# First attention of a two-layer kernel: outputs sent through DRAM to the projection, and an unread 26-row product after the second scores

## What is computed

```python
qkv = x @ qkv_w + qkv_b
qkv = qkv.reshape(b, n, 3, H, D)              # b 16, n 512, H 16 heads, D 8
q, k, v = jnp.moveaxis(qkv, 2, 0)
attn = jnp.einsum('bnhd,bmhd->bhnm', q, k) * scale
attn = jax.nn.softmax(attn, axis=-1)
out = jnp.einsum('bhnm,bmhd->bnhd', attn, v).reshape(b, n, c)
out = out @ proj_w + proj_b                   # and x = x + out
```

## Time and profile before

| | us |
|---|---|
| median of 3 runs | 3365.65 |
| lowest, highest | 3340.04, 3366.84 |
| the profiled execution | 3353.67 |
| its span | 3351.9 |
| stretch of the first attention in it | about 460 to 1337 |
| mean granted TensorE clock over the span | 0.908 |

### The profile page before, as it was taken

The page is one execution under the profiler, slowest core; times in us unless marked ns, Lnnn a source line. Parts: engine busy times, 40 slices in busy tenths (PEclk is TensorE's granted clock), DMA queues, the critical chain, the costliest instruction groups (busy, mean ns, idle before and its releaser), DMA issues. The chain is left out here.

```text
span 3351.9 us, 46625 instructions
## 1 busy us (share of the span) xinstructions
PE 2934.7 (88%) x15938; PEld 1757.2 (52%) x15938; DVE 2516.6 (75%) x6115; ACT 1773.0 (53%) x2711; POOL 928.1 (28%) x885
## 2 busy tenths in 40 slices
PE   6999959999999998899995689899799999989853
PEld 4666623443443443666663556566566666656432
DVE  6888767888888880788876797867366778797765
ACT  3444406777777775444435556454345555555544
POOL 2221121121111100212101355556323323343333
PEclk9999957999999996899995689989899999999965
DMA  4343432122122110343430000000000000000000
GB/s 127 77 100 80 95 102 93 57 93 84 66 93 84 66 49 6 111 93 79 101 77 1 1 7 20 19 19 19 32 13 13 13 7 14 13 7 26 7 7 25
DMA packets 71588, 167.20 MB, mean 50 GB/s; under 512 B 8792, under 2 KB 9400, under 8 KB 67128
## 3 DMA queue, kind: packets, MB, share of 16 engines
q1 hardware_dynamic: 69176, 160.03, 16.5%
q10 hardware_dynamic: 2176, 4.19, 0.3%
HBM read 120.67 MB, written 43.52 MB: 49 GB/s over the span
## 5 line engine op out<-in xcount | busy, mean ns | idle before, releaser
L706 DVE TENSOR_REDUCE att_mx<-att_pair 128x2 f32<-128x1024 f32 x512 | 617.0, 1220 | 132.5 <-PE att_pair L955 132.1
L881 ACT ACTIVATE att_pt<-att_pair 128x1024 f32<-128x1024 f32 x512 | 522.8, 1025 | 235.7 <-PE att_pair L965 233.1
L977 PE MATMUL att_o<-att_pt,att_vx 128*32 128x256 f32 x4096 | 335.5, 413 | 9.8 <-ACT att_oT L887 5.1
L955 PE MATMUL att_pair<-att_k,att_q 24*128 24x512 f32 x1024 | 272.4, 535 | 48.8 <-DMA att_k<-att_spread_k 14.2
L965 PE MATMUL att_pair<-att_q,att_k 26*128 26x512 f32 x1024 | 265.5, 520 | 0.0
L965 PEld LDWEIGHTS att_pair<-att_q,att_k 26*128 26x128 f32 x1024 | 98.5, 191 | 195.0 <-issue 168.1
L457 ACT ACTIVATE ffnA_h<-ffnA_up,b 128x512 f32<-128x512 f32 x144 | 98.7, 686 | 178.9 <-PE ffnA_up L105 177.2
L457 ACT ACTIVATE ffnB_h<-ffnB_up,b 128x512 f32<-128x512 f32 x144 | 98.6, 685 | 178.1 <-PE ffnB_up L105 176.4
L955 PEld LDWEIGHTS att_pair<-att_k,att_q 24*128 24x128 f32 x1024 | 100.3, 195 | 136.2 <-ACT att_pt L881 89.2
L977 PEld LDWEIGHTS att_o<-att_pt,att_vx 128*32 128x32 f32 x4096 | 91.6, 111 | 143.0 <-issue 123.4
L1897 ACT ACTIVATE att1k_sq<-att1k_k 128x512 f32<-128x512 f32 x128 | 76.2, 595 | 165.0 <-PE att1k_k L105 164.9
(11 more groups left out here) (538 smaller groups left out, 7787.8 us busy)
## 6 DMA issues: line engine op xcount, KB each, us to landing
ffnA_weights<-ffnA_weights SPq DMA_DIRECT2D x128, 256.0 KB, 5.6
att_q<-att_spread_q SPq DMA_DIRECT2D x16, 1024.0 KB, 4.9
att_k<-att_spread_k SPq DMA_DIRECT2D x16, 1024.0 KB, 4.8
att_spread_q<-att_qhi SPq DMA_DIRECT2D x32, 256.0 KB, 2.5
att_spread_k<-att_khi SPq DMA_DIRECT2D x32, 256.0 KB, 3.3
twk_hi<-ffnB_weights SPq DMA_DIRECT2D x32, 256.0 KB, 3.9
twk_lo<-ffnB_weights SPq DMA_DIRECT2D x32, 256.0 KB, 5.0
tgk_hi<-ffnB_weights SPq DMA_DIRECT2D x32, 256.0 KB, 6.0
```

Source lines behind the costliest of these rows:

```text
L706: v.tensor_reduce(top[b % 2][:, t, h:h + 2], pair("s", k)[:, :].rearrange("p (h n) -> p h n", h=2), AX, ALU.max, negate=True).then_inc(mx, 1)
L881: a.activation(pt[k % 8][:, :, :].rearrange("p h n -> p (h n)"), pair("t", k)[:, :], ACT.Exp, scale=scale).then_inc(p_, 1)
L955: last = pe.matmul(pair("s", k)[:, (j - j0) * 512:(j - j0 + 1) * 512], qb[b % 3][r, u, t * P:(t + 1) * P], kb[b % 3][r, u, :], start=True, ...
L977: last = pe.matmul(obank[j * BLOCK:(j + 1) * BLOCK, cols], vxb[b % 3][:, t, 4 * u + j, :], pt[(2 * g + j // 2) % 8][:, j % 2, cols], start ...
```

## The change

The outputs are no longer turned on TensorE. ACT issues a DMA (`kept`, at 6, 14, 22, 30) that stores each unit's `oT` in DRAM, in `heads_o`, one row for each head and value. When a group's four units are there, SP (`gathered`) reads the 16 rows of sums as 128 x 64 and the 128 rows of numerators as 128 x 512. DVE takes the reciprocal of the sums at 19 (`inverted`), SP (`returned`) writes it to DRAM and reads it back with each head's row on eight partitions, and POOL multiplies into `ocol` (`divided`). The projection moves to 26, the addition to 28. With that `out`, `final` and their users are gone from the order of `misc`.

`misc_idle` lists for each step in which no user of `misc` is due the user that comes next: from two steps after a user to the step before the next. In a full group these are the steps 4, 7, 8, 11, 12, 15, 16, 19 to 25 and 28 to 33 (33 is step 1 of the next pass). There `keep_clock` runs one more matmul like the second scores, at row block 0, into `misc`, where nobody reads it. It stands between `again` and `scores`, and waits through `misc_free` as the next user would. POOL now runs the split of the next group's q and k before the norm of the group after it, and SP's queue takes `gathered` between the q and the k operands and `returned` behind the k operands.

```diff
     def uses_of_misc():
-        yield from (("x", 0), ("q", 0), ("k", 0), ("v", 0))
+        yield from ((-1, "x", 0), (-1, "q", 0), (-1, "k", 0), (-1, "v", 0))
...
             if now:
-                yield "maxima", m - 1
+                yield STEPS * m + 2, "maxima", m - 1
             if new:
-                yield "x", m + 1
+                yield STEPS * m + 5, "x", m + 1
+                yield STEPS * m + 9, "q", m + 1
+                yield STEPS * m + 13, "k", m + 1
+                yield STEPS * m + 17, "v", m + 1
...
+                yield STEPS * m + 26, "proj", m - 2
+
+    misc_order = list(uses_of_misc())
+    misc_uses = [(kind, k) for _, kind, k in misc_order]
+    misc_idle = {step: (kind, k) for (last, _, _), (next_, kind, k) in zip(misc_order, misc_order[1:]) for step in range(max(last, 0) + 2, next_)}
...
+        def inverted(b):
+            v.wait_ge(dsum, 16 * (b + 1))
+            if b:
+                v.wait_ge(wr, 16 * b)
+            v.reciprocal(rec[:, :], sums[:, :]).then_inc(turned_over, 1)
...
-                if n == 24 and old:
+                if n == 28 and old:
                     ended(m - 2)
...
+        def divided(b):
+            p.wait_ge(dnum, 16 * (b + 1))
+            p.wait_ge(drec, 16 * (b + 1))
+            if b:
+                p.wait_ge(fp, b)
+            p.tensor_tensor(ocol[:, :], num[:, :], recb[:, :], ALU.mult).then_inc(weighted, 1)
...
+        for m in range(groups + 2):
+            if m + 1 < groups:
+                spread(m + 1)
+            if m >= 2:
+                divided(m - 2)
+            if m + 2 < groups:
+                normal(m + 2)
...
+        def gathered(b):
+            for written in wo:
+                sp.wait_ge(written, 16 * UNITS // 2 * (b + 1))
+            sp.dma_start(sums[:, :], heads_o[:, HDIM, :].rearrange("h (a n) -> h a n", n=FOLD)).then_inc(dsum, 16)
+            if b:
+                sp.wait_ge(weighted, b)
+            sp.dma_start(num[:, :], heads_o[:, 0:HDIM, :]).then_inc(dnum, 16)
+
+        def returned(b):
+            sp.wait_ge(turned_over, b + 1)
+            if b:
+                sp.wait_ge(drec, 16 * b)
+            sp.dma_start(spread_r.rearrange("h (a n) -> (h a) n", n=FOLD), rec[:, :]).then_inc(wr, 16)
+            sp.wait_ge(wr, 16 * (b + 1))
+            if b:
+                sp.wait_ge(weighted, b)
+            sp.dma_start(recb[:, :], spread_r.unsqueeze(1).to_broadcast([HEADS, HDIM, GROUP])).then_inc(drec, 16)
...
             if m + 1 < groups:
-                operands(m + 1)
+                operands_q(m + 1)
+            if m >= 2:
+                gathered(m - 2)
+            if m + 1 < groups:
+                operands_k(m + 1)
+            if m >= 2:
+                returned(m - 2)
...
         def out(w):
             a.wait_ge(w_, 2 * TILES * (w + 1))
             if w >= 2:
-                a.wait_ge(oTT, w - 1)
+                a.wait_ge(wo[w % 2], 16 * (w // 2))
             a.activation(oTb[w % 2][:, :], obank[:, :], ACT.Copy).then_inc(oT, 1)
...
+        def kept(w):
+            b, u = divmod(w, UNITS)
+            a.wait_ge(oT, w + 1)
+            if u == 0 and b:
+                a.wait_ge(dsum, 16 * b)
+                a.wait_ge(dnum, 16 * b)
+            a.dma_start(heads_o[4 * u:4 * u + 4].rearrange("j r n -> (j r) n"), oTb[w % 2][:, :]).then_inc(wo[w % 2], 16)
...
+        def keep_clock(k):
+
+            step = k + LAG
+            if step in misc_idle:
+                b, u, t, _ = place(k)
+                r = slice(0, SHIFTED)
+                misc_free(pe, *misc_idle[step])
+                pe.matmul(misc[:, :], kb[b % 3][r, u, t * P:(t + 1) * P], qb[b % 3][r, u, :], start=True, stop=True)
...
-        def out(w):
-            pe.wait_ge(oT, w + 1)
-            misc_free(pe, "out", w)
-            turn_back(pe, misc, oTb[w % 2], ident).then_inc(oTT, 1)
-
-        def final(b):
-            pe.wait_ge(on, UNITS * (b + 1))
-            misc_free(pe, "final", b)
-            turn(pe, misc, group(otok[b % 2][:, :]), ident).then_inc(fT, 1)
-
         def projected(b):
-            pe.wait_ge(fc, b + 1)
+            pe.wait_ge(weighted, b + 1)
...
                 if 0 <= k < total:
                     again(k)
+                    keep_clock(k)
                 if STEPS * m + n + 1 < total:
                     scores(STEPS * m + n + 1)
...
-                if n == 23 and old:
+                if n == 26 and old:
                     projected(m - 2)
```

More of the change, by code:

```diff
@@ L612, in attn0 @@
     oTb = mem.ring("oT", 2, [P, GROUP])
-    rec = mem.ring("rec", 2, [P, TILES, 4])
-    otok = mem.ring("otok", 2, [P, GROUP])
+    sums, rec = mem.sb("sums", [P, FOLD]), mem.sb("rec", [P, FOLD])
+    num, recb = mem.sb("num", [P, GROUP]), mem.sb("recb", [P, GROUP])
     ocol = mem.sb("ocol", [P, GROUP])
@@ L755, in vector @@
                     maxima(m - 1)
[L756 to L759, removed]
+                if n == 19 and old:
+                    inverted(m - 2)
                 if n == 20 and m + 2 < groups:
@@ L794, in normal @@
             p.tensor_tensor(xg(b), xg(b), A["pb"][:, :].unsqueeze(1).to_broadcast([P, TILES, C]), ALU.add).then_inc(biased, 1)
-        for b in range(groups):
-            normal(b)
-            spread(b)
+        def divided(b):
[4 more added lines that the diff above has]
+            p.tensor_tensor(ocol[:, :], num[:, :], recb[:, :], ALU.mult).then_inc(weighted, 1)
+        normal(0)
+        spread(0)
+        if groups > 1:
+            normal(1)
+        for m in range(groups + 2):
[5 more added lines that the diff above has]
+                normal(m + 2)
     def sync(sp):
@@ L908, in scalar @@
                     out(UNITS * (m - 2) + 2)
+                if n == 6 and old:
+                    kept(UNITS * (m - 2) + 2)
                 if n == 6 and new:
@@ L914, in scalar @@
                     out(UNITS * (m - 2) + 3)
+                if n == 14 and old:
+                    kept(UNITS * (m - 2) + 3)
                 if n == 14 and new:
@@ L920, in scalar @@
                     out(UNITS * (m - 1))
-                if n == 22 and old:
-                    final(m - 2)
+                if n == 22 and now:
+                    kept(UNITS * (m - 1))
                 if n == 29 and now:
                     out(UNITS * (m - 1) + 1)
+                if n == 30 and now:
+                    kept(UNITS * (m - 1) + 1)
     def tensor(pe):
@@ L1024, in tensor @@
                     turned(m + 1)
-                if n == 7 and old:
-                    out(UNITS * (m - 2) + 2)
                 if n == 9 and new:
@@ L1030, in tensor @@
                     project_k(m + 1)
-                if n == 15 and old:
-                    out(UNITS * (m - 2) + 3)
                 if n == 17 and new:
                     project_v(m + 1)
-                if n == 21 and old:
-                    final(m - 2)
-                if n == 23 and old:
+                if n == 26 and old:
                     projected(m - 2)
-                if n == 25 and now:
-                    out(UNITS * (m - 1))
-                if n == 30 and now:
-                    out(UNITS * (m - 1) + 1)
     with nc.Block() as block:
```

60 lines of the change are left out of this document (14 added, 46 removed).

## The result

| | before | after |
|---|---|---|
| median | 3363.7 us (3340.0 to 3366.8, 4 runs) | 3494.3 us (3482.2 to 3499.2, 4 runs) |
| ratio to before, 95% interval | | 1.040 (1.034 to 1.045) |
| span of the profiled execution | 3351.9 us | 3489.6 us |

A forecast was written before the change was run, and what follows sets the result against it. Each 49.8 us group period was taken as the loop of second scores, exponential and first scores plus PE's misc work. +3 + 33 - 1.3 - 23 + 7 = +18.7 us gave 3371; forecast 3375, range 3335 to 3420.

The forecast's parts named there:

- The sum in the attention: First attention: changes of all its groups, drain and tail added up to +18.7 us, of which groups 2 to 14 +33.
- Rival B: Drain of the first attention: the clock is not held, drain +8 us instead of -23, whole kernel 3406 us; chance 0.25.
- The drain: End of the first attention, without first scores: 42 steps at full clock take 51 us instead of 74, -23 us.
- Group 15: Last group of the first attention, without x, q, k, v: loses the turnings, gets the product's runs, -1.3 us.
- The loop and the misc work: Group period: 16 step pairs of 2.62 us plus PE's other work; with the change 53.0 us instead of 49.8.
- The 47.6: Group period in us after removing turnings (46.9) and adding ACT's store issues (0.7), before the unread product's 5.4.
- Rival C: Unread product: costs no array time, only waits; period 50.6 us, whole kernel 3344 us; chance 0.12.
- Rival D: Unread product: its waits don't show, ACT's copies running ahead; period 47.6 us, whole kernel 3305 us; chance 0.08.
- ACT's stores: Four DMA issues a group in ACT's queue: those at steps 6 and 14 cost 0.35 us each, 0.7 a period.
- The way through DRAM: Stores and reads of outputs and sums in each group: fit the DMA share and arrive in time, counted as nothing.
- rival E: DRAM chain comes late for step 19 or 26, or holds SP's k operands; whole kernel 3415 us; chance 0.06.
- the tail: End of the first attention, last output copy to last addition: 13.3 us instead of 6.25, with four DMAs; +7 us.

The follow-up runs named there:

- e8b: The kernel before with only one of four transposes in each of its five turnings of outputs, and division on that tile alone: 3377.3 us, ratio 1.008.
- e5: The changed kernel with five unread turnings a group, behind the weighing, in place of its 20 products: 3384.8 us, ratio 1.013.
- e13: The changed kernel with two 128 x 128 transposes in place of each unread product, same steps and waits: 3489.1 us, ratio 1.039.
- e4: The changed kernel with all its unread products moved behind the first scores and weighing of their step: 3445.0 us, ratio 1.030.
- e9: The changed kernel with 128-row x 256-column products only at six odd idle steps and in the drain: 3440.7 us, ratio 1.027.
- e10: The kernel before with an unread float32r product of 128 rows x 256 columns at the drain's idle steps: 3385.7 us, ratio 1.010.
- e6: The changed kernel with five unread products of 128 rows x 512 columns a group in place of its 20 products: 3426.6 us, ratio 1.020.
- e12: The kernel before with two unread float32 products of 128 rows x 128 columns at each idle step of the drain: 3357.1 us, ratio 1.000.
- e2: The changed kernel without the unread product but with its waits on the shared bank kept: 3459.8 us, ratio 1.035.
- e3: The changed kernel with the unread product only in the drain, nowhere else: 3431.0 us, ratio 1.027.
- e1: The changed kernel without the unread product and its waits, outputs still going through DRAM: 3407.5 us, ratio 1.020.

## Why the prediction was wrong

**The step that failed** stands in "The sum in the attention": "+33; that the 8 us of lower clock go is taken in". It priced 13 periods at 53.0 us with the clock at 1.00. I had taken the turnings out as 2.95 us of PE time, and put the product in as something that could only help the clock. Both the sign and the size were wrong: the mean clock of these groups fell from 0.98 to 0.81. The runs showed that the turnings had helped to hold it (e8b with nothing else of the change, e5, and e13, where transposes for the products bring back 0.96), and that the 26-row product does not replace them (e4). The price is 83.5 us in twelve groups. Of whole-array products e9 and e10 held none of it; e6 and e12 leave open whether some is held.

**Rival B** had the clock fall in the drain, with the price of a drain alone. No rival had it fall in the middle. A sign was in my own rows: in the drain the clock stood at 0.51 with PE busy all of the time, so a busy PE was no promise of the full clock. I used that for the drain and not for the middle, where five of the seven turnings were about to go.

**The drain**, -23 forecast, is +4: the clock was 0.64. **Group 15**, -1.3 forecast, is +7, at a clock of 0.75 instead of 0.93.

**The loop and the misc work** came near: 53.0 forecast, 51.74 at full clock. Its parts are less sure than the sum. The late copy, half a microsecond behind the free bank, and the second product on the same row block 0.34 us behind the first stand in the timeline of step 7. PE idles 2.4 us a group ahead of the products, where 3.0 were forecast. e2, without array time, gave 49.9 where 50.6 stood. The 47.6 from which the sum starts no run shows by itself: e3, which has no product in the middle, takes 48.8, with PE waiting for POOL for 20.7 us in 13 groups, 1.6 each; less that, it is about 47.2, an estimate. Rival C, no array time, is out, since 51.74 lies 1.8 us above e2. Rival D, hidden waits, is out: the 31.5 us of idle PE are there.

**ACT's stores**: 0.33 us an issue, as SP's row said. **The way through DRAM** was in time in this kernel: in groups 2 to 14 DVE has no wait for the sums, and the projection none for POOL (rival E), so only the tail pays, 14.25 us against 13.3. It was in time by the slowness of the rest: with the shorter periods of e1, e3 and e5 the projection does wait. The term that I had put at nothing would have cost something in a kernel that met the forecast of rivals C or D. The four DMAs of the tail, at 2.0 us each in the sum, took 8.9: the small write of the reciprocals was through 1.5 us after its issue (1468.49 to 1469.97), the broadcast read took 3.3 us (1469.97 to 1473.31). The Trainium skill, DMA: Bandwidth & Descriptors, section Anatomy of one DMA, gives 2.0 us + bytes / 436 GB/s for DMAs on GpSimd's path. An estimate with it for these four, which ACT and SP issue, is 9.4 us, and 14.7 for the tail. The trace's 8.9 lies between, but neither rule has the 3.3 us of the broadcast read.

**What stays open.** Why transposes hold the clock: the kind of instruction, its operand (the identity) and how it is run (the traces show two matmuls for each float32 product of e12, one for each transpose) were not told apart. A whole-array product, float32 above all, was never tried at the steps of e13, and e12's executions disagree with its profile. Why five unread turnings (e5) gave 0.93 and not the 0.98 of before, and whether waits (for POOL in e1 and e5, for the bank in e2 and in e13's drain at 0.80) take some of the clock. The spread of the middle from run to run is as large as most of these differences. Nor is the count of transposes the whole of it: the drain before has 32 of them in 73.2 us and stands at 0.67, the middle of the kernel after 8 in each 59.7 us at 0.81.

## What to carry to other kernels

Before taking an instruction off TensorE, look at the granted clock of stretches with a different mix of instructions, and don't take a busy PE for a promise: here it stood at half clock while busy all the time. Price a change of PE's work twice, once at full clock by its loop and waits, and once by the us that may go to the lower clock, in this kernel at about 0.35 us each. And a filler meant to hold the clock has to be measured as one, for its clock and not only its time: here the cheap one that shared the array did nothing. Last, when an experiment takes something out, look at its waits too: e1 removed one kind and got another.

## What the runs showed of the hardware

In these kernels float32 transposes of 128 x 128 held TensorE at 2.4 GHz better than products did. In the drain of before, which has eight turnings of its own, with a filler at 26 of its 42 steps and PE busy 97 to 99% of it in e10 to e12: four transposes 0.97, two 0.97 (PE busy 95%), one 0.77, two float32 products of 128 columns 0.68, one float32r product of 128 rows x 256 columns 0.62, no filler 0.67. Each is one profile; against it stands e13's drain, 0.80 with two transposes. In the changed kernel's middle, two transposes in place of each 26-row product: 0.96 instead of 0.81. At full clock, four products on four different row blocks take no longer than two (0.43 us to the weighing, which uses all four), while two on the same block start 0.34 us apart (865.34 and 865.68 in step 7 of the kernel after).
